# Attention's dot products by seven block products inside the last layer's blocks, and one load of weights' rows issued sooner

## The reference

```python
xn = layernorm(x)
dot_products = xn @ (xis[:, None] * proj_matrix).T          # 256 features
feats   = 1/16 * exp(xis) * exp(dot_products - 0.5 * sum(xn * xn) * xis**2)
weights = the same of input_weights
s = feats @ weights.T
h = silu(xn @ w1.T * w1_s) * (xn @ w2.T * w2_s)              # 1024 wide
h = gelu(h @ h1.T * h1_s);  h = gelu(h @ h2.T * h2_s)
out = x + s * silu(h @ w3.T * w3_s)
```

## Time and profile before

| | |
|---|---|
| median of 3 runs | 1304.79 us |
| profiled execution | 1305.41 us, its span 1303.6 us |
| TensorE (PE) busy | 1293.0 us, 99% of the span |
| weight loads (PEld) | 1071.2 us, 82% |
| VectorE (DVE) | 938.6 us, 72% |
| GpSimd (POOL) | 781.9 us, 60% |
| ScalarE (ACT) | 751.8 us, 58% |
| mean granted TensorE clock | 0.999 |

### The profile page before, as it was taken

The page is one execution under the profiler, slowest core; times in us unless marked ns, Lnnn a source line. Parts: engine busy times, 40 slices in busy tenths (PEclk is TensorE's granted clock), DMA queues, the critical chain, the costliest instruction groups (busy, mean ns, idle before and its releaser), DMA issues.

```text
span 1303.6 us, 16286 instructions
## 1 busy us (share of the span) xinstructions
PE 1293.0 (99%) x6092; PEld 1071.2 (82%) x6092; DVE 938.6 (72%) x1202; ACT 751.8 (58%) x1003; POOL 781.9 (60%) x803
## 2 busy tenths in 40 slices
PE   9999999999999999999999999999999999999997
PEld 7778888888888887888878888788887888878887
DVE  7878758777587775878668686777858777456675
ACT  4556645666456664465645656456555566455664
POOL 7973015899569994699946998378984790040000
PEclk9999999999999999999999999999999999999999
DMA  9698835545264541654517454275442754313441
GB/s 339 256 354 245 290 118 147 188 155 177 76 174 153 177 163 69 171 180 147 166 65 201 151 173 139 81 189 169 160 129 81 205 163 138 105 65 129 141 164 38
DMA packets 98197, 209.61 MB, mean 161 GB/s; under 512 B 14144, under 2 KB 17472, under 8 KB 97088
## 3 DMA queue, kind: packets, MB, share of 16 engines
q1 hardware_dynamic: 80176, 157.11, 36.1%
q0 software_dynamic: 17936, 51.39, 14.2%
HBM read 175.92 MB, written 38.83 MB: 165 GB/s over the span
## 4 chain that ended last, share of the span: by engine, by line
PE 98%; DVE 1%; ACT 0%; issue 0%; POOL 0%; POOLq 0%
PE ps L222 74%; PE ps L225 23%; DVE split L205 1%; DVE quad L205 0%; ACT split L201 0%; PE ps L353 0%; ACT quad L201 0%; PE ps L237 0%; DVE ry L205 0%; DVE xin L205 0%; ACT xT L201 0%; POOL ident L549 0%; POOL ident L546 0%; POOL ones L547 0%; POOLq L549 0%
## 5 line engine op out<-in xcount | busy, mean ns | idle before, releaser
L222 PE MATMUL ps<-split,ring 128*128 128x512 f32 x2800 | 763.8, 390 | 1.1 <-DVE split L205 1.1
L222 PEld LDWEIGHTS ps<-split,ring 128*128 128x128 f32 x2800 | 525.5, 188 | 110.6 <-DVE split L205 1.6
L205 DVE TENSOR_TENSOR split<-quad,split 128x1024 fp32r<-128x1024 f32 x258 | 340.8, 1331 | 186.7 <-ACT split L201 185.6
L225 PE MATMUL ps<-split,ring 128*128 128x512 f32 x784 | 305.0, 389 | 0.0
L201 ACT ACTIVATE split<-quad 128x1024 fp32r<-128x1024 f32 x258 | 266.3, 1052 | 43.9 <-PE ps L225 43.9
L222 PE MATMUL ps<-xT,w 128*128 128x512 f32 x766 | 220.2, 395 | 0.8 <-ACT xT L201 0.8
L648 POOL TENSOR_TENSOR cube<-cube,seen 128x256 f32<-128x256 f32 x176 | 208.9, 1187 | 14.1
L201 ACT ACTIVATE quad<-ps 128x512 f32<-128x512 f32 x193 | 114.4, 596 | 118.3 <-PE ps L225 118.3
L201 ACT ACTIVATE quad<-quad,cols 128x512 f32<-128x512 f32 (+1 forms) x194 | 137.5, 717 | 64.1 <-DVE quad L205 63.8
L222 PEld LDWEIGHTS ps<-xT,w 128*128 128x128 f32 x766 | 143.1, 188 | 35.6 <-issue 3.3
L225 PEld LDWEIGHTS ps<-split,ring 128*128 128x128 f32 x784 | 147.2, 188 | 30.6
(11 more groups left out here) (104 smaller groups left out, 1210.5 us busy)
## 6 DMA issues: line engine op xcount, KB each, us to landing
ring<-hs SPq DMA_DIRECT2D x428, 256.0 KB, 3.5
xin<-in_x SPq DMA_DIRECT2D x16, 512.0 KB, 3.3
s_h<-s SPq DMA_DIRECT2D x16, 512.0 KB, 5.8
seen<-in_h POOLq DMA_DIRECT2D x64, 128.0 KB, 2.8
ry<-in_x SPq DMA_DIRECT2D x15, 512.0 KB, 6.0
out<-ry SPq DMA_DIRECT2D x15, 512.0 KB, 2.6
z_h<-xin POOLq DMA_DIRECT2D x56, 128.0 KB, 4.4
xT<-z_h POOLq DMA_DIRECT2D x14, 512.0 KB, 7.0
```

The source lines that it names most:

```text
L205: return dve.mark(lambda e: e.tensor_tensor(dst, a, b, op))
L222: pe.run(lambda e: e.matmul(dst, stat, mov, start=start, stop=stop, skip_group_check=loose))
L225: return pe.mark(lambda e: e.matmul(dst, stat, mov, start=start, stop=stop, skip_group_check=loose))
```

## The change

From tile 1 on the dot products of both halves are taken together as one 2x2 block product: PT has blocks a11, a21, a12, a22, the rows have b11, b21 (the first half's two input blocks) and b12, b22 (the second half's). Seven products p1 to p7 of fp32 blocks replace the eight. They need four sums of PT's blocks (once, `sums_of_proj`, in the new buffer `PS`), three of the rows' blocks (`sums_of_rows`, t1, t2 and, in place of b12, t3) and t4 later. The products are no longer at the tile's start: each is written out behind every second block of `down` of the tile before (`beside`). Banks 4, 5 and 6 hold them; ScalarE copies (c11, u2, u3) take intermediate states of bank 4 into the features' buffer. The exponents are made by VectorE in between, the exponential at the tile's start (`features_of`, one instruction a half). Tile 0 keeps `dots`.

The second part: `load(7)` is issued inside `make(5)`, after the third of its four sums, where it stood behind `make(5)`.

```diff
+        PS = sb("PS", [P, 4, P])
...
+        def sums_of_rows(h0):
+            h1 = h0 + 1
+            b11, b12, b22 = xTf[0][:, 0, :], xTf[1][:, 0, :], xTf[1][:, 1, :]
+            t1, t2 = stage[0][:, :], stage[1][:, :]
+            a = summed[1] = vv(t1, b12, b11, ALU.subtract, xTf_done[h0], xTf_done[h1], *stage_free[0])
+            summed[2] = vv(t2, b22, t1, ALU.subtract, a, *stage_free[1])
+            summed[3] = vv(b12, b22, b12, ALU.subtract, *xT_hi[h1], xT_lo[h1], summed[2])
...
+            def p1():
+                tok = plain(PT[:, 0, 0:P], xTf[0][:, 0, :], A, True, False, xTf_done[h0], *free[banks[0]])
+                box["c11"] = cast(q[0, 0], A, tok, *quad_free[place])
+            def p2():
+                tok = plain(PT[:, 1, 0:P], xTf[0][:, 1, :], B, True, True, *free[banks[1]])
+                a = vv(q[0, 0], B, q[0, 0], ALU.add, tok, box["c11"])
+                free[banks[1]] = [a]
+                exponent(0, 0, q[0, 0], a)
+            def p6():
+                tok = plain(PS[:, 1, :], stage[1][:, :], A, False, False, summed["S"], summed[2], box["c11"])
+                box["u2"] = cast(q[0, 1], A, tok)
+                box["t4"] = vv(stage[1][:, :], xTf[0][:, 1, :], stage[1][:, :], ALU.subtract, tok)
+            def p5():
+                tok = plain(PS[:, 0, :], stage[0][:, :], E, True, False, *free[banks[2]])
+                stage_free[0] = [tok]
+                box["p5"] = tok
+            def p7():
+                tok = plain(PS[:, 2, :], xTf[1][:, 0, :], A, False, False, summed[3], box["u2"])
+                u3 = box["u3"] = cast(q[1, 1], A, tok)
+                a = box["c22"] = vv(q[1, 1], E, q[1, 1], ALU.add, box["p5"], u3)
+                exponent(1, 1, q[1, 1], a)
+            def p4():
+                tok = plain(PT[:, 1, P:2 * P], stage[1][:, :], A, False, True, box["t4"], box["u3"])
+                stage_free[1] = [tok]
+                exponent(1, 0, A, tok)
+                free[banks[0]] = [box[1, 0]]
+            def p3():
+                tok = plain(PS[:, 3, :], xTf[1][:, 1, :], E, False, True, box["c22"])
+                a = vv(q[0, 1], E, q[0, 1], ALU.add, tok, box["u2"])
+                free[banks[2]] = [a]
+                exponent(0, 1, q[0, 1], a)
+                xin_free[0] = xin_free[1] = [tok]
+                for j in range(2):
+                    qrow_free[j] = [box[r, j] for r in range(KD)]
+            return [p1, p2, p6, p5, p7, p4, p3]
+
+        def features_of(h, place):
+            j = h % 2
+            here = quad[place][:, KD * j:KD * j + KD, :]
+            feat[h] = cast(here, here, *seven[h], func=ACT.Exp)
...
                 both(a11, a22, a11, ALU.subtract)
+                if beside is not None:
+                    load(beside)
                 both(a12, a12, a11, ALU.subtract)
...
-            make(5)
-            load(7)
+            make(5, 7)
...
                     if last:
                         y_done[2 * t + j, b] = tok
+                    if b % 2 and beside:
+                        beside.pop(0)()
...
-                dots(h0, (4, 5), L0.at["v"])
-                dots(h1, (2, 3), L0.at["v"])
+                features_of(h0, L0.at["v"])
+                features_of(h1, L0.at["v"])
...
+                (4, 2): [sums_of_proj] if t == 0 else [lambda: sums_of_rows(h0 + 2)] if t + 1 < NT else [],
...
+            beside = []
+            if t + 1 < NT:
+                if t == 0:
+                    sums_of_rows(h0 + 2)
+                beside = seven_dots(h0 + 2, next_at["v"], (4, 5, 6))
+            down(t, C, between, beside)
```

More of the change, by code:

```diff
@@ L453, in dots, with sums_of_proj @@
             xin_free[j] = [tok]
+        seven, summed = {}, {}
+        def sums_of_proj():
+            a11, a12, a21, a22 = (PT[:, k, r * P:(r + 1) * P] for r in range(2) for k in range(2))
+            S1, S2, S3, S4 = (PS[:, i, :] for i in range(4))
+            a = vv(S1, a21, a22, ALU.add, made_w["PT"])
+            vv(S3, a11, a21, ALU.subtract)
+            a = vv(S2, S1, a11, ALU.subtract, a)
+            summed["S"] = vv(S4, a12, S2, ALU.subtract, a)
+        def sums_of_rows(h0):
[5 more added lines that the diff above has]
+            summed[3] = vv(b12, b22, b12, ALU.subtract, *xT_hi[h1], xT_lo[h1], summed[2])
@@ new lines, in seven_dots, with plain, exponent @@
+        def seven_dots(h0, place, banks):
+            h1 = h0 + 1
+            A, B, E = (ps[:, bank, :] for bank in banks)
+            q = {(r, j): quad[place][:, KD * j + r, :] for r in range(KD) for j in range(2)}
+            box = {}
+            def plain(weights, moving, dst, first, last, *tokens):
+                pe.wait(*tokens)
+                return mm_mark(dst, weights, moving, first, last, True)
+            def exponent(r, j, src, *tokens):
+                dst = q[r, j].rearrange("p (b q) -> p b q", b=NB)
+                box[r, j] = vst(dst, qrow[j][:, :].rearrange("p (q b) -> p b q", b=NB), ab2[:, r:r + 1],
+                                src.rearrange("p (b q) -> p b q", b=NB), ALU.mult, ALU.add, *tokens, qrow_done[h0 + j])
+                seven[h0 + j] = seven.get(h0 + j, []) + [box[r, j]]
+            def p1():
[33 more added lines that the diff above has]
+            return [p1, p2, p6, p5, p7, p4, p3]
@@ L599, in both, with make @@
                 pool.wait(pool.mark(lambda e: e.tensor_tensor(dst, a, b, op)))
-            def make(n):
+            def make(n, beside=None):
                 layer, k = todo[n]
@@ L863, in y_place, with down @@
             return 2 * (h % 2) + b // 2, (b % 2) * D
-        def down(t, C, between):
+        def down(t, C, between, beside):
             order = ORDER if t + 1 < NT else ORDER_END
@@ L1055, in build @@
                 (3, 0): [split(L1, "t3", 0)], (3, 1): [split(L1, "t3", 1)], (3, 2): [sub(L1, "t4", 1)], (3, 3): [split(C, "b11", 0, 2)],
-                (4, 0): [split(L1, "b22", 0)], (4, 1): [split(L1, "b22", 1)], (4, 3): [split(C, "b11", 1, 2)] + first(norms_in, h0 + 2) + first(norms_in, h1 + 2),
+                (4, 0): [split(L1, "b22", 0)], (4, 1): [split(L1, "b22", 1)], (4, 2): [sums_of_proj] if t == 0 else [lambda: sums_of_rows(h0 + 2)] if t + 1 < NT else [],
+                (4, 3): [split(C, "b11", 1, 2)] + first(norms_in, h0 + 2) + first(norms_in, h1 + 2),
                 (5, 0): [split(L1, "t4", 0)], (5, 1): [split(L1, "t4", 1)], (5, 2): first(turn_blocks, h0 + 2), (5, 3): first(split_rows, h0 + 2),
@@ L1080, in between @@
                     store_y(h1)
-            down(t, C, between)
+            beside = []
[4 more added lines that the diff above has]
+            down(t, C, between, beside)
+            assert not beside
         h = 2 * NT - 2
```

## The result

The changed kernel takes 1296.62 us (median of 6 runs, 1295.85 to 1297.24) against 1304.80 (6 runs, 1304.42 to 1304.96): a ratio of 0.9938 with a 95% interval of 0.9927 to 0.9948, or 8.2 us. The profiled execution took 1296.85 us, its span 1295.0 (before 1303.6).

What follows compares the result with a forecast made beforehand. TensorE was taken as the bound, busy 1293.0 of 1303.6 us. From the profiled 1305.41, -6.0 for products and +0.5 for stalls gave 1299.9, as a median 1299.3; range 1297.8 to 1302.4.

Steps and rivals of the forecast that it cites:

- What TensorE saves: Dot products of tiles 1 to 7: seven in place of eight, each priced 0.86 us, saving 6.0 us.
- What a lone product costs at its edges: Down stage: entering and leaving a product set between w3's blocks costs 0, at most one exposed weight load of 0.19.
- The three sums at (4, 2): VectorE sums before product 4's third sum, second hidden layer: slack 1.67, TensorE waits 0.1 in each of five tiles.
- the 0.5 us that I added for five tiles: Stall allowed at the seventh product because the sums at (4, 2) collide with GpSimd, 0.1 a tile.
- rival B: Sums at (4, 2) collide with GpSimd, t4's split comes late: stalls in five tiles, 1301.3 to 1307.3 us; chance 0.15.
- the worst case: At (4, 2) each sum waits out a whole GpSimd instruction: stall 1.6 in five tiles, 8 us, about 1307; chance 0.03.
- The eighth block's load: Tile 0: load issued some 2.4 us earlier, no gain of its own; effect on TensorE's 1.13 us wait taken as 0.
- the whole 1.13 gone: Favourable bound for tile 0's one TensorE wait on a VectorE split; the other bound was as much again.
- The new chain in the down stage: Copies, sums and exponents between products: all seven waits done before TensorE arrives, least slack 1.1 us, costing nothing.
- Rivals C and D: C: lone products lose time at edges, up to 1317; D: down-stage copies over 1.1 late, 1305.1 at 2; chance 0.05 each.
- The sum: Profiled 1305.41 less 6.0 plus 0.5 gives 1299.9; the median being 0.6 below, 1299.3 us.

Runs made afterwards that it cites:

- E2: The changed kernel with the eighth load put back behind make(5), so the seven products alone: 1298.05 us, ratio 0.9947.
- E3: The kernel before with its eight dot products set singly between down-stage blocks, no product less, no sums, one exponential a half: 1306.74 us, ratio 1.0015.
- E7: As E3 on the kernel before, but the eight lone dot products each one block sooner: 1303.88 us, ratio 0.9993.
- E4: The changed kernel with three more VectorE sums at (4, 2) in tiles 1 to 6, into a buffer nothing reads: 1310.66 us, ratio 1.0045.
- E6: The kernel before with the eighth load inside make(6), after three of its four sums: 1303.76 us, ratio 0.9991.
- E9: The changed kernel with the eighth load moved into make(6), after three of its four sums: 1296.42 us, ratio 0.9937.
- E5: The kernel before with the eighth load inside make(5) after two of its four sums: 1304.89 us, ratio 1.0002.
- E1: The kernel before with only the load moved, into make(5) after three of its four sums: 1303.44 us, ratio 0.9991.
- E10: The changed kernel with the eighth load back in its old place, run again on one chip with E9 and E11: 1298.46 us, ratio 0.9951.
- E11: The whole change run again, on one chip with E9 and E10: 1296.91 us, ratio 0.9941.
- E8: The changed kernel with its seven products each one block sooner in the down stage: 1296.87 us, ratio 0.9941.

## Why the prediction was wrong in size

**What TensorE saves: the mechanism right, the term too small.** "7 x 0.86 = 6.0 us" measured 6.9 in the trace (0.98 a tile) and 6.65 in E2's runs. The step that failed here is the rate: it priced the product left out and let the seven that remain cost what they cost in a row. By E3 and E7, the same eight matmuls set singly between w3's blocks save 0.09 to 0.10 in the down stage: a lone product takes 0.848 and one in the row 0.86. The rest, 0.98 - 0.10, is one lone product and a remainder of 0.03. The remainder comes in the gated steps that follow: at 680.50, where the kernel before is at 686.21, TensorE is 0.99 ahead, counted from the stage's start, and it was 0.93 to 0.94 ahead at the second gated group. Why it comes there, and why a lone product takes less than one in the row, no run shows.

**What a lone product costs at its edges: right that it loses nothing.** I took 0 with a bound of a loss; it was a small gain, the one above, for which the bounds made no room.

**The three sums at (4, 2): nearly right.** Forecast: two of three collide, +0.53 each, TensorE waits 0.13. Measured: two of three collide, +0.43 each, and 0.50 of slack is left, so the 0.5 us that I added for five tiles were not there. Of the 0.63 between these, 0.2 is the smaller growth and 0.2 an idle stretch of VectorE ahead of t4's first low (628.98 to 629.20 before) that I had not counted; the rest is not worked out. E4 shows that rival B's mechanism is real and how near it was: 3.2 us more work a tile cost 14 us in all.

The rule of the Trainium skill ("SBUF — State Buffer", section "Who interferes with whom") agrees in when such collisions come: operations with one operand in PSUM kept 0.68 there, operations with both in SBUF grew beside GpSimd and, in tile 6, did not. I read the 0.53 of the earlier trace rows as less than the rule's whole instruction. The rows don't set the two apart: a sum that comes while GpSimd's instruction is under way stands out only the rest of it. The first of the two longer sums came 0.57 before GpSimd's instruction ended and ended 0.55 after it, 1.12 in place of 0.69; the other is the same within 0.01. The same holds for the 1.75 of the earlier trace rows: of the 133 operations of 1024 elements that took over 1.3 us in the trace of before, 92 end 1.1 after a GpSimd instruction's end and 29 end 0.6 after one. So the worst case was too dark because it let every sum come at an instruction's start.

**The eighth block's load: a term put at nothing.** "No gain of its own ... I take 0" was right that the data's landing is of no use: E6 and E9 issue it 6 and 8 us later than what they are compared with and are as good as the place of the change, E5 issues it sooner and gains nothing. But the bound that I named, "the whole 1.13 gone", is what happened, and more: 1.3 us alone (E1) and 1.55 beside the products (E10, E11). The trace of before had the rows for it: VectorE's two lows there took 1.77 and 2.72 against 1.22 elsewhere, so some 2 us of collision stood on the path of TensorE's one wait. The bound itself was too small by 0.3, since it took the wait for its row. I should have laid the moved DMA issue, 1.05 long, beside these lows in time, as I did with the sums at (4, 2).

**The new chain in the down stage: right.** Its times came out within 0.7 us, most within 0.2, and E8 finds no wait in it. Rivals C and D did not come.

**The sum.** 6.9 + 1.4 (tile 0, between E1's 1.3 and E10's 1.55) = 8.3 against 8.2 measured. Of the 2.7 us between this and the forecast, 0.9 are the seven tiles, 1.3 to 1.55 tile 0's wait, 0.5 the stall that did not come. The range's lower end, 1297.8, already had the wait's 1.13 gone and no stall; the 1.2 below it are the rate (0.9) and what the wait cost beyond its row (0.3).

## What to carry to other kernels

When TensorE is the bound, price a change of order as carefully as a change of work: also the matmuls that only move to other neighbours. A DMA issue on GpSimd takes time on that engine's list, and moving it moves all the sums behind it; lay the new times beside VectorE's instructions with two SBUF operands before calling it nothing. Price a wait of TensorE by the starts of the matmuls around it and not by its row alone. Before moving products to the end of a stage, follow the last one's exponent and exponential into the next stage's first steps: one product fewer left this change a whole pair of blocks there, and eight in the same places, with one long exponential a half (E3), lost more than the place gave.

## What the runs showed of the hardware

- An fp32 product of 128x128 by 512 columns takes 0.848 us singly between blocks of 256-column fp32r matmuls (if these keep their pace), 0.86 in a row of its kind; alternating the two kinds 49 times showed no cost.
- A wait of TensorE that its row gives as 1.13 us cost 1.43 by the starts and lengths of the records around it; two of 1.41 and 0.81 made a tile 2.8 longer (E4).
- VectorE's 512-element sums with both operands in SBUF took 0.69 without GpSimd's arithmetic and, beside it, 0.68, 1.12 and 1.11, the long ones ending 0.55 after GpSimd's instruction. 1024-element lows took 1.22 alone; those that stood out a GpSimd sum of 512 elements ended 1.08 or 1.09 after its end (before and E1 at 69.55 and 68.68, E5 at 67.01).
- Which of the two goes first is not settled by the order of starts in the records: a low that began 0.12 after a GpSimd sum took 2.28 (E5), one that began 0.57 ahead of the next took 1.23 (E1), but one that began 0.33 ahead took 2.72 (before). What decides is open.
